# Conv-style attention with relative positions, two layers, on one Trainium2 core: the Sync queue reads q and k back after the maxima, xd and the output; score products one slot later

## The chip, the cores and the metric

The kernel runs on one core of one Trainium2 chip. The metric is the device time of one execution, in microseconds; lower is better.

## The reference

Two layers of the same shape, each `x = x + attention(groupnorm(x))`, on 64 samples of 14 x 14 tokens with 192 channels. Group normalisation takes 32 groups of 6 channels over the whole sample. The attention has 12 heads of 16 channels and a decomposed relative-position bias:

```python
q, k, v = (qkv[0], qkv[1], qkv[2])                 # qkv = gn(x) @ qkv_w + qkv_b
attn  = einsum('bqd,bkd->bqk', q * scale, k)
rel_h = einsum('bhwc,hkc->bhwk', q_as_grid, Rh)    # Rh[i,j] = rel_pos_h[i-j+H-1]
rel_w = einsum('bhwc,wkc->bhwk', q_as_grid, Rw)
attn  = softmax(attn + rel_h[..., :, None] + rel_w[..., None, :])
out   = (attn @ v) @ proj_w + proj_b
x     = x + out
```

Every product and sum above is computed for all 64 samples in both layers, and the second layer normalises what the first one has written.

## The kernel before, in words

One **unit** is one sample in one layer, so there are 128 units. The five engines each run their own program over all units. The work is software-pipelined by hand. Time is cut in iterations of 12 **slots**, one per head, and each step of a unit has a slot number counted from the unit's own iteration: slot number `at` is carried out in iteration `i` for unit `i - at // 12`, at position `at % 12`. On one engine, position and the order of the statements inside a position fix the order of instructions. Slots tie no engine to another; only semaphores do. So a slot number matters by the order that it gives on its queue.

What a unit goes through, with the lines of the profile:

- SP (SyncE's DMA queue) brings the sample in, `xa` (L395). PE transposes it, `xT` (L430), ACT and DVE copy it out and take the statistics (L739, L744), POOL turns them into scale and shift and writes the normalised sample as a high and a low half-precision part (`xn_hi`, `xn_lo`, L839, L844).
- PE forms q and k (`qk0`, `qk1` jobs, L413, slot 3), ACT and DVE write them as high and low parts `qk_hl` (L600, L730). SP writes them to DRAM (`qk_out`, L342: q first, then k) and reads them back in another layout into `q_st` and `k_st` (`q_in`, L370; `k_in`, L376, two transfers). v is formed in slot 10 (L413).
- PE forms the relative-position products (`rel0`, `rel1`, `rel2`, L474), ACT and DVE write them as `rel_hl`, and SP copies them into further rows of `q_st` (`rel`, L359, four transfers).
- From slot 28 on, one head per slot: PE forms the scores for the maxima (L525), DVE reduces them (`mx`, L718). After six heads PE transposes the maxima (`mT0`, `mT1`, L480), ACT writes them negated as `mrow` (L612), and SP puts them in the last row of `q_st` (`m0` and `m1`, L337). `m0` is for heads 0 to 5, `m1` for heads 6 to 11.
- From slot `EXP_AT` on, one head per slot: PE forms the score products again (L538), now with the maximum as one more row, and ACT takes the exponential (L588) into `probs`. Before head 0 PE waits for `m0`'s transfer, before head 6 for `m1`'s. PE multiplies probabilities and v (`PV_AT`, L557) in groups of four heads. The first group starts in slot 44 and waits for the exponential of head 3.
- The result is transposed (`ot`, L491, `oT`, L501), projected (`y`, L413, slot 60), and POOL adds the residual `xd` (L383) to it (`yo`, L855). SP writes `yo` out (`out`, L388). POOL's program has the statistics of the next unit (`mv`, L802, L805), which wait for DVE's L744, ahead of `yo` in each iteration.

PE works through its slots strictly in order. In one position it takes the maxima's product (L525), then the score product (L538), then the jobs of that position, then probabilities and v. ACT has in each position first the copy of L557's result, then the exponential, then the other copies.

SP's loop tests the steps in this order at each position: `m0`, `m1`, `rel`, `qk_out`, `q_in`, `k_in`, `xd`, `out`, `xa`. Each `dma_start` there stands behind its wait, and SP goes on only when that wait is over. With the numbers of before (`i` the iteration) SP's order in one iteration is: `xa(i+1)`, `m0(i-3)`, `qk_out(i)`, `q_in(i)`, `k_in(i)`, `xd(i-4)`, `out(i-5)`, `m1(i-3)`, `rel(i-1)`. `q_in` waits until q has landed in DRAM, `k_in` until k has, `out` for `yo` of its own unit, `m1` for ACT's `mrow`, `rel` for DVE's last part.

Of the kernel before, what the change touches and what calls it, by code (L numbers as in the profile page):

```python
# [71 lines left out]
def attention_kernel(nc, x_in, w_all, b_qk, b_rows, rel, onehot, lo_rows, ident_in, gmat_in, out):  # L72
    with ExitStack() as ctx:
# [42 lines left out]
        def pair(name, shape, dt=F32):  # L116
            return [sb(f"{name}{i}", shape, dt) for i in range(2)]

        xa = pair("xa", [HT, 2, C])
# [25 lines left out]
        xd = pair("xd", [HT, 2, C])  # L145
# [98 lines left out]


        LEAD, TAIL = 1, 6
        MAX_AT, EXP_AT = 28, 40

        PV_AT = {(0, 0): 44, (0, 1): 45, (1, 0): 49, (1, 1): 51, (2, 0): 54, (2, 1): 54}
        O_LATER = 1  # L250
# [22 lines left out]
        POOL_AT = {"mv": -11, "group": -3, "xn": -1, "xhi": 0, "xlo": 0, "y": 63}  # L273
        QK_TILES = ((0, 1), (2,))

        SP_AT = {"m0": 39, "m1": 46, "rel": 22, "qk_out": 3, "q_in": 3, "k_in": 4, "xd": 55, "out": 69, "xa": -12}

        def head_at(base, slot):

# [2 lines left out]
        def due(unit, slot, at):  # L282

            u = unit(at // HEADS)
            return u if at % HEADS == slot and active(u) else None
# [23 lines left out]
        def _(sp):  # L309
# [23 lines left out]
            def maxima(unit_, half):  # L333

                if active(unit_):
                    wait(sp, s_mrow, unit_.n * 2 + half + 1)
                    sp.dma_start(q_st[unit_.r][R_MAX:STACK, half * HH:half * HH + HH, :, :],  # L337
                                 mrow[unit_.r % 2][:, half, :]).then_inc(s_m[half][unit_.r], 16)

            def to_dram(unit_, dram, row, landed):  # L340

                sp.dma_start(dram[unit_.r].rearrange("l d h c t -> (d h) l (c t)"),  # L342
                             qk_hl[unit_.r % 2][row:row + HQ * HD, :, :, :]
                             .rearrange("p l c t -> p l (c t)")).then_inc(landed[unit_.r], 16)

            def iteration(unit, layer):
                for s in range(HEADS):
                    for half in range(2):
                        u = due(unit, s, SP_AT[f"m{half}"])
                        if u:  # L350
                            maxima(u, half)
                    u = due(unit, s, SP_AT["rel"])
                    if u:
                        wait(sp, s_rlo, u.n * 3 + 3)
                        for axis in range(2):
                            rows = RW if axis == 0 else 2 * SIDE
                            for half in range(2):
                                p, r0 = 64 * axis + 32 * half, R_REL + RW * axis
                                sp.dma_start(q_st[u.r][r0:r0 + rows, half * HH:half * HH + HH, :, :],  # L359
                                             rel_hl[u.r % 2][p:p + rows, :, :]).then_inc(s_rel[u.r], 16)  # L360
                    u = due(unit, s, SP_AT["qk_out"])
                    if u:
                        wait(sp, s_qklo, u.n * 2 + 2)
                        to_dram(u, q_dram, 0, s_qd)
                        to_dram(u, k_dram, HQ * HD, s_kd)
                    u = due(unit, s, SP_AT["q_in"])
                    if u:
# [3 lines left out]
                          .then_inc(s_qst[u.r], 16)  # L371
                    u = due(unit, s, SP_AT["k_in"])
                    if u:
                        wait_dma(sp, s_kd, u)
                        for part in range(2):
                            sp.dma_start(k_st[u.r][2 * HD * part:2 * HD * part + 2 * HD, :, :],  # L376
                                         k_dram[u.r].rearrange("l d h c t -> d l (h c t)"))\
                              .then_inc(s_kst[u.r], 16)
                    u = due(unit, s, SP_AT["xd"])
                    if u:  # L380
# [533 lines left out]
```

## Time and profile before

| | us |
|---|---|
| median of 3 runs (2547.81 to 2555.18) | 2550.9 |
| the profiled execution | 2526.95 |
| its span, first to last instruction | 2525.2 |
| PE busy | 2178.0 (86%) |
| DVE busy | 1434.6 (57%) |
| ACT busy | 1419.7 (56%) |
| POOL busy | 715.6 (28%) |
| mean granted TensorE clock | 0.879 |

A profile's row for a group of instructions gives the line, the engine, the operation, the tiles, how often it ran, how long it was busy and what ended the idle time before it. A row of a timeline gives start, duration, engine, line, operation and tiles, and in brackets the idle time before it with what ended it. PE's durations are modelled: the start of the next matmul tells more than the duration of the last. The granted clock is 1.00 at 2.4 GHz and 0.50 at 1.2 GHz.

### The profile page before, as it was taken

The page shows a single profiled execution, that of the slowest core. Times are in us where ns is not written, and L with a number is a line of the kernel's source. Part 1 is how long each engine was busy: PE and PEld are TensorE (multiplying, and loading weights), DVE is VectorE, ACT ScalarE, POOL GpSimd, SP SyncE. Part 2 cuts the span into 40 slices and gives each one's busy share as a digit, 9 for nine tenths or more (in the row PEclk, how much of TensorE's full clock was granted, in tenths as well). Part 3 has the DMA queues.
Part 4 walks back from the last instruction along what each step waited for, and adds up shares of the span by engine and source line. Part 5 has one row for each costly group of instructions (what it writes and reads, how often), then busy time and mean ns, then how long its engine had stood idle before and what let it go on. Part 6 is the DMA issues. An engine that isn't in the chain of part 4 may idle for free.

```text
span 2525.2 us, 86928 instructions
## 1 busy us (share of the span) xinstructions
PE 2178.0 (86%) x35072; PEld 1815.6 (72%) x35072; DVE 1434.6 (57%) x3540; ACT 1419.7 (56%) x3329; POOL 715.6 (28%) x1796
## 2 busy tenths in 40 slices
PE   2888888888988888988988888988888888898897
PEld 2777777777777777776777777777777777777776
DVE  5655555565555556555555555655555655565554
ACT  1556555555655555655555555555555655565555
POOL 1322322232223223223222322332223222323220
PEclk9989888888888989989888988888888988998888
DMA  2433333333333334333333433333333333333331
GB/s 49 106 85 84 93 85 85 83 98 87 80 85 90 92 81 100 86 85 98 84 80 85 101 81 80 90 92 85 80 90 95 85 87 81 96 90 88 89 78 52
DMA packets 170599, 217.20 MB, mean 86 GB/s; under 512 B 29783, under 2 KB 138072, under 8 KB 170202
## 3 DMA queue, kind: packets, MB, share of 16 engines
q1 hardware_dynamic: 170202, 211.64, 33.8%
q8 instruction: 282, 4.62, 0.8%
q14 instruction: 115, 0.94, 0.1%
HBM read 117.00 MB, written 57.80 MB: 69 GB/s over the span
## 4 chain that ended last, share of the span: by engine, by line
PE 42%; DMA 30%; SPq 16%; DVE 5%; issue 3%; ACT 3%; POOL 1%; POOLq 0%; ACTq 0%
PE ps_m L413 21%; DMA q_st<-mrow 14%; DMA k_dram<-qk_hl 10%; PE ps_sc L538 8%; SPq L376 7%; PE ps_max L525 6%; DMA q_dram<-qk_hl 5%; DVE qk_hl L730 4%; SPq L383 3%; PE ps_m L501 3%; SPq L388 3%; PE ps_o L557 3%; ACT qk_hl L600 2%; SPq L342 2%; SPq L370 1%
## 5 line engine op out<-in xcount | busy, mean ns | idle before, releaser
L718 DVE TENSOR_REDUCE mx<-ps_max 98x2 f32<-98x392 f32 x1536 | 836.8, 562 | 433.1 <-PE ps_max L525 431.4
L588 ACT ACTIVATE probs<-ps_sc 98x392 f32<-98x392 f32 x1536 | 727.7, 495 | 536.6 <-PE ps_sc L538 505.5
L538 PE MATMUL ps_sc<-q_st,k_st 125*98 125x196 f16 x3072 | 568.7, 270 | 286.4 <-DMA q_st<-mrow 286.1
L525 PE MATMUL ps_max<-k_st,q_st 124*98 124x196 f16 x3072 | 580.4, 273 | 0.9 <-DVE mx L718 0.7
L538 PEld LDWEIGHTS ps_sc<-q_st,k_st 125*98 125x98 f16 x3072 | 352.7, 137 | 314.3 <-DMA q_st<-mrow 311.6
L525 PEld LDWEIGHTS ps_max<-k_st,q_st 124*98 124x98 f16 x3072 | 324.5, 135 | 204.7 <-issue 198.3
L802 POOL TENSOR_TENSOR msq<-mv 96x2 f32<-96x2 f32 x128 | 24.6, 192 | 1538.2 <-DVE mv L744 1538.2
L557 PE MATMUL ps_o<-probs,v_st 98*32 98x196 f32 x6144 | 389.0, 340 | 0.5 <-ACT o_sb L578 0.5
L636 ACT ACTIVATE rel_hi<-ps_m,is_lo 128x504 f16<-128x504 f32 (+1 forms) x384 | 225.8, 588 | 149.4 <-PE ps_m L474 137.3
L776 DVE TENSOR_TENSOR oT_lo<-ps_m,oT_hi 96x392 f16<-96x392 f32 x128 | 71.9, 562 | 415.5 <-ACT oT_hi L618 415.5
L474 PE MATMUL ps_m<-q_st,rel_st 64*32 64x36 f16 (+1 forms) x14336 | 238.2, 209 | 1.9 <-DVE rel_hl L769 1.6
L769 DVE TENSOR_TENSOR rel_hl<-ps_m,rel_hi 128x504 f16<-128x504 f32 (+1 forms) x384 | 216.2, 563 | 23.2 <-ACT rel_hi L636 6.5
L474 PEld LDWEIGHTS ps_m<-q_st,rel_st 64*32 64x32 f16 x14336 | 191.5, 101 | 46.1 <-DVE rel_hl L769 2.3
L413 PE MATMUL ps_m<-xn_hi,w_hi 98*128 98x196 f16 (+1 forms) x768 | 193.2, 252 | 10.4 <-POOL xn_lo L844 10.4
L413 PE MATMUL ps_m<-xn_lo,w_hi 96*128 96x196 f16 x768 | 192.2, 250 | 0.0
L730 DVE TENSOR_TENSOR qk_hl<-ps_m,qk_hl 128x392 f16<-128x392 f32 (+1 forms) x256 | 107.2, 460 | 149.5 <-ACT qk_hl L600 149.5
L413 PE MATMUL ps_m<-xn_hi,w_lo 96*128 96x196 f16 x768 | 191.6, 249 | 0.0
L557 PEld LDWEIGHTS ps_o<-probs,v_st 98*32 98x32 f32 x6144 | 134.4, 108 | 73.2 <-issue 1.0
L413 PE MATMUL ps_m<-w_hi,xn_lo 96*98 96x192 f16 x512 | 176.0, 344 | 0.0
L413 PE MATMUL ps_m<-w_lo,xn_hi 96*98 96x192 f16 x512 | 175.8, 343 | 0.0
L413 PE MATMUL ps_m<-w_hi,xn_hi 98*98 98x192 f16 (+1 forms) x512 | 175.6, 343 | 0.0
L413 PE MATMUL ps_m<-w_hi,oT_hi 98*98 98x192 f16 (+1 forms) x512 | 154.0, 301 | 2.7 <-DVE oT_lo L776 2.7
(72 smaller groups left out, 3338.3 us busy)
## 6 DMA issues: line engine op xcount, KB each, us to landing
q_st<-q_dram SPq DMA_DIRECT2D x128, 294.0 KB, 3.9
k_st<-k_dram SPq DMA_DIRECT2D x256, 147.0 KB, 3.9
q_dram<-qk_hl SPq DMA_DIRECT2D x128, 147.0 KB, 2.6
k_dram<-qk_hl SPq DMA_DIRECT2D x128, 147.0 KB, 2.7
q_st<-rel_hl SPq DMA_DIRECT2D x256, 73.5 KB
q_st<-rel_hl SPq DMA_DIRECT2D x256, 64.3 KB
xa<-in_x SPq DMA_DIRECT2D x64, 147.0 KB
xd<-in_x SPq DMA_DIRECT2D x64, 147.0 KB
```

Source lines behind the costliest of these rows:

```text
L376: sp.dma_start(k_st[u.r][2 * HD * part:2 * HD * part + 2 * HD, :, :], k_dram[u.r].rearrange("l d h c t -> d l (h c t)"))\
L383: sp.dma_start(xd[u.r % 2][:, :, :], tokens(src[bass.ds(at, 1)])).then_inc(s_xd[u.r], 16)
L413: last = nc.tensor.matmul(dst, weights(a, c, k), moving(b, c, k), start=n == 0, stop=n == len(terms) - 1)
L474: last = nc.tensor.matmul(to, rel_st[:, lay, axis, w:w + RW], q, start=True, stop=True)
L525: last = nc.tensor.matmul(ps_max[head % 2][0:HT, h * TOK:h * TOK + TOK], q_st[u.r][0:R_MAX, head, h, :], k_st[u.r][0:R_MAX, head, :], star ...
L538: last = nc.tensor.matmul(ps_sc[head % 2][0:HT, kt * TOK:kt * TOK + TOK], k_st[u.r][0:STACK, head, kt * HT:kt * HT + HT], q_st[u.r][0:STAC ...
L557: last = nc.tensor.matmul(ps_o[32 * j:32 * j + 32, 0:TOK], v_st[u.r][:, kt, head_of(head), :], p[:, kt, :], start=kt == 0, stop=kt == 1)
L588: nc.scalar.activation(probs[head][:, :, :], ps_sc[head % 2][0:HT, 0:2 * TOK].rearrange("p (k t) -> p k t", k=2), ACT.Exp, scale=1.0 / (QS ...
L636: nc.scalar.activation(rel_part(rel_hi[u.r % 2], n), rel_bank(n), ACT.Identity, scale=is_lo[:, 0:1]).then_inc(s_rhi, 1)
L718: nc.vector.reduce_max(mx[u.r % 2][:, head, :], ps_max[head % 2][0:HT, 0:2 * TOK].rearrange("p (q k) -> p q k", q=2), axis=AX.X).then_inc( ...
L730: nc.vector.tensor_tensor(qk_hl[u.r % 2][:, 1, at, :], ps_m[BANK[f"qk{j}"]][:, 0:len(tiles) * TOK].rearrange("p (c t) -> p c t", t=TOK), q ...
L769: nc.vector.tensor_tensor(rel_part(rel_hl[u.r % 2], n), rel_bank(n), rel_part(rel_hi[u.r % 2], n), ALU.subtract).then_inc(s_rlo, 1)
```

## The change

Only slot numbers change. SP's order becomes `xa(i+1)`, `m0(i-3)`, `qk_out(i)`, `xd(i-4)`, `out(i-5)`, `m1(i-3)`, `q_in(i)`, `k_in(i)`, `rel(i-1)`. `m0` keeps its place in the order, and so do `qk_out`, `rel` and `xa`. The score products and exponentials of each head are one slot later on PE and ACT. No instruction is added or removed.

```diff
-        MAX_AT, EXP_AT = 28, 40
+        MAX_AT, EXP_AT = 28, 41
...
-        SP_AT = {"m0": 39, "m1": 46, "rel": 22, "qk_out": 3, "q_in": 3, "k_in": 4, "xd": 55, "out": 69, "xa": -12}
+        SP_AT = {"m0": 37, "m1": 43, "rel": 22, "qk_out": 4, "q_in": 8, "k_in": 8, "xd": 54, "out": 66, "xa": -12}
```

## Rows read from the trace of the kernel before

**Rows 1.** Waits over the whole span: engine, line, releaser: total us, times, longest us

```profile
PE ps_sc L538 <- DMA q_st<-mrow: 286.1, 125, 3.7
```

**Rows 2.** Span and mean granted clock of the core

```profile
core 0: 2525.2 us, clock 0.879
```

**Rows 3.** The chain that ended last, one iteration: start us, us, what

```profile
1209.63 2.80 DMA k_dram<-qk_hl
...
1215.53 2.19 DMA q_st<-mrow
```

**Rows 4.** PE timeline, an iteration at the full clock, 860 to 879 us

```profile
860.42 0.37 PE L538 MATMUL ps_sc<-q_st,k_st 125*98 125x196 f16 x2 [2.03 <-DMA q_st<-mrow]
...
866.95 0.50 PE L430 MATMUL ps_m<-ident,xa 98*96 98x98 f32 x4
...
877.12 0.37 PE L538 MATMUL ps_sc<-q_st,k_st 125*98 125x196 f16 x2 [1.75 <-DMA q_st<-mrow]
...
878.66 0.33 PE L525 MATMUL ps_max<-k_st,q_st 124*98 124x196 f16 x2
```

**Rows 5.** One-us windows, 1216 to 1225 us: PE busy (matmuls), granted clock, DMA share, GB/s

```profile
1216.00:1217.00 1.00, 0.27 (x2) 1.00 0.81 266
...
1218.00:1219.00 1.00, 1.00 (x8) 0.50 0.32 78
...
1224.00:1225.00 1.00, 1.00 (x14) 0.78 0.02 2
```

**Rows 6.** SP's own timeline in the same iteration as rows 4

```profile
868.02 0.68 SPq L342 DMA_DIRECT2D q_dram<-qk_hl  x1
868.74 0.64 SPq L342 DMA_DIRECT2D k_dram<-qk_hl  x1
870.63 0.56 SPq L370 DMA_DIRECT2D q_st<-q_dram  x1
871.32 1.41 SPq L376 DMA_DIRECT2D k_st<-k_dram  x2
872.77 0.57 SPq L383 DMA_DIRECT2D xd<-in_x  x1
873.39 0.41 SPq L388 DMA_DIRECT2D x<-yo  x1
873.85 0.81 SPq L337 DMA_DIRECT2D q_st<-mrow  x1
874.71 2.90 SPq L359 DMA_DIRECT2D q_st<-rel_hl  x4
877.65 0.55 SPq L395 DMA_DIRECT2D xa<-in_x  x1
```

**Rows 7.** POOL timeline of the iteration after, whose L430 on PE started at 883.65

```profile
887.31 1.00 POOL L855 TENSOR_TENSOR yo<-yr,xd 98x384 f32<-98x384 f32 x1
```

**Rows 8.** The page's group of the exponentials: busy, mean ns, idle before

```profile
L588 ACT ACTIVATE probs<-ps_sc 98x392 f32<-98x392 f32 x1536 | 727.7, 495 | 536.6 <-PE ps_sc L538 505.5
```

**Rows 9.** PE timeline around slot 44: what stands between head 4's scores and L557

```profile
1232.49 1.18 PE L491 MATMUL ps_m<-ident,o_sb 128*98 128x68 f32 x12
...
1234.04 0.54 PE L557 MATMUL ps_o<-probs,v_st 98*32 98x196 f32 x8
```

**Rows 10.** SP's issues of k's read-back, 147 KB each: ns and landing us, min/median/max

```profile
L376 SPq DMA_DIRECT2D k_st<-k_dram x256: 552/593/1724, 50.3 to 2466.9; - x128
...
DMA to landing us min/median/max: 2.8/3.9/5.0
```

**Rows 11.** SP's issues of rel: ns min/median/max

```profile
L359 SPq DMA_DIRECT2D q_st<-rel_hl x512: 536/783/1449, 64.4 to 2488.9; - x171
```

**Rows 12.** Half-us window behind rows 6 (same columns as rows 5)

```profile
880.50:881.00 0.50, 0.50 (x10) 1.00 0.00 0
```

**Rows 13.** PE timeline: first and last of the 125 waits of rows 1

```profile
93.68 0.37 PE L538 MATMUL ps_sc<-q_st,k_st 125*98 125x196 f16 x2 [1.02 <-DMA q_st<-mrow]
...
2471.93 0.56 PE L538 MATMUL ps_sc<-q_st,k_st 125*98 125x196 f16 x2 [3.39 <-DMA q_st<-mrow]
```

## The prediction, made before the changed kernel had run

> **What bounds the kernel now.** I read the totals of the waits first. PE has one large wait: the score products of head 6 wait for the transfer of `m1`, the second row of maxima, 125 times, 286.1 us in all, 2.3 us a unit [rows 1]. PE is busy for 86% of the span and every other engine for 57% or less, so PE's own order of work is the frame and this wait is the hole in it.
>
> The chain that ended last says why `m1` is late. One iteration of it runs from the q and k products over `qk_hl` and SP's write to DRAM, the landing of k there (2.80 us), the read-backs, `xd`, `out` and `m1` to the landing of `m1` (2.19 us), and only then into L538 [rows 3, 4]. The maxima are not late. SP stands in front of them, because `q_in` and `k_in` wait for landings and `m1` is behind them.
>
> SP's timeline shows this in numbers. I count from the start of `xT` on PE (L430, 866.95, [rows 4]), which follows the q and k products directly, and call it zero. `qk_out` is issued from 1.07 to 2.43, `q_in` starts at 3.68 when q has landed, `k_in` at 4.37, `xd` at 5.82, `out` at 6.44, `m1` at 6.90, `rel` at 7.76 and `xa` at 10.70 [rows 6]. L538 of head 6 starts at 10.17, after 1.75 us of waiting, that is, PE was there at 8.42 [rows 4].
>
> The windows show a second price. The clock is granted in full while PE stands still and falls to half right behind it: 1.00 at 1216, 0.50 at 1218, back only during 1224 [rows 5]. The mean of 0.879 [rows 2] puts 2 x 0.121 x 2525.2 = 611 us at 1.2 GHz. In the one-us windows of the whole span I find falls only behind such a wait, never in the busy stretches between two of them. Some waits are followed by none, and one such case is in [rows 4]. There one iteration is 877.12 - 860.42 = 16.70 us, of which 1.75 is the wait: **14.95 us of PE work at the full clock**. The average iteration between the first and the last wait is (2471.93 - 93.68) / 124 = 19.18 us [rows 13]. The difference of 4.23 us is 2.3 us of waiting and 1.9 us of slow clock.
>
> **The change, part by part.**
>
> *SP's order.* Nothing is added, so the issues keep their durations and only their order is new. `xd` can go at 2.47 (its own wait is for a residual sum two units back, long over) and is done at 3.04. `out` now waits for something: `yo` of its unit ends on POOL at 888.31, which is 4.66 after that iteration's `xT` [rows 7]. So `out` is issued from 4.70 to 5.11 and `m1` from 5.15 to 5.96. Its landing after the start of the issue took 3.27 us in one iteration (873.85 to 877.12, [rows 4, 6]), and 2.19 in another [rows 3]. That gives a landing between 7.4 and 8.4. I take 7.9, between them; both ends go into the range.
>
> *Behind `m1`.* `q_in` goes at 6.0, and q landed before 3.7, so its old wait is gone. `k_in` runs from 6.6 to 8.1. k's landing in DRAM, from 1.79 with 2.8 us [rows 3], is over at 4.6; with the 5.0 us that is the longest landing of a 147 KB transfer [rows 10] it would be over at 6.8, 0.2 late. The four `rel` transfers take 2.90 and end at 11.0, `xa` at 11.6. Against before, `xa` starts at 11.05 instead of 10.70, 0.35 later. First users: `q_in` is needed by `rel0` in the next iteration, over 5 us after its landing; `k_in` an iteration after that; `rel` by the next maxima's head 0 behind `xT`, at about 15.9. The tightest is `xa`, needed at 14.95 by the next `xT`. Its landing isn't listed. The DMA engines stand still at 880.5 [rows 12], 2.85 us after `xa`'s issue at 877.65 [rows 6], so it lands by 13.9, with 1.05 to spare. With 5.0 us [rows 10] it would be 16.05, 1.1 late. I take 2.85, since it is of this transfer itself, and keep the other end. `m0`, behind `xa`, lands by 11.6 + 3.3 = 14.9 and is needed at about 16.4.
>
> *Scores one slot later.* PE now has one more score product, `oT` and the v product in front of head 6. Everything from head 6's scores to the next maxima's product takes 878.66 - 877.12 = 1.54 us [rows 4], and one more maxima's product follows (0.17). So PE needs `m1` at 8.42 + 1.54 + 0.17 = 10.1 instead of 8.42. Against the landing of 7.4 to 8.4 that is 1.7 to 2.7 us of slack, while with the new order alone it would be 0 to 1.0. The slot costs little otherwise. In slot 44 the scores of head 3, not 4, now stand in front of L557, which needs that head's exponential of 0.495 us [rows 8]. Between them PE still has `ot` and `rel2`, 1234.04 - 1232.49 = 1.55 us [rows 9]. If that cover were gone, the cost would be some 0.5 us in each of 128 units, 64 us. The pipeline's end is one slot longer, 0 to 1 us once.
>
> *The sum.* Up to the first wait's start: 93.68 - 1.02 = 92.7. Then 124 x 14.95 = 1853.8. Behind the last one, 2525.2 - 2471.93 = 53.3, less 3.2 for a slow stretch behind it like the one in [rows 5] (6.4 us at half the clock, from 1218 to 1224.4): 50.1. Half a us for the slot. Together **1997.1 of span**, 1999 with the 1.75 us around the span. The profiled execution (2526.95) lies 24 us, 0.9%, under the median of 2550.9. I expect most of that spread to come from the waits and the clock and little to stay; with a few us for scattered late transfers I forecast **2004**. A cross-check from the totals gives 2525.2 - 286.1 - 611/2 = 1934. It is too low, as part of the slow clock falls into the waits, where it costs nothing, but it marks the low end.
>
> **The clock.** The fall comes behind the wait [rows 5], and without a fall PE needs 14.95 us [rows 4]. By these rows the clock comes back with the wait gone. The Trainium skill (TensorE: Matmul & The Clock Gate, "HAM oscillation — how this bites in real kernels") ties the fall to an idle gap longer than 1.75 us; by that rule the waits would not be its cause, and removing them would not cure it.
>
> **The rivals.**
>
> *The clock doesn't return.* Only the wait goes: 2525.2 - 286.1 + 1.75 = 2241. For it speaks that the cause of a fall is inferred, and that not every wait has one. Against it, that no fall in the trace stands away from a wait. Chance 0.06. That is the time that the sentence of the Trainium skill above would give.
>
> *The wait moves to `xa`.* SP's order now closes a loop: `xa` releases `xT`, its statistics release POOL's `yo`, this releases `out`, and behind `out` stand `m1`, `q_in`, `k_in`, `rel` and the next `xa`. The loop is 13.9 us by my sums, only 1.05 under PE's 14.95. Issues and landings that are a little longer when the same traffic fits into 15 instead of 19 us make some iterations end on it. At 16.05 in every iteration it is 124 x 1.1 = 136 us, 2140; short waits that also halve the clock could bring it to 2230. Chance 0.12.
>
> *Slower.* The same loop at its worst. `k_in` with both issues at 1.72 (2.0 more than in [rows 6], by [rows 10]), `rel` with four at 1.45 (2.9 more, [rows 11]) and a landing of 5.0 (2.15 more) make 13.9 + 7.05 = 20.9 us, 124 x 20.9 + 143 + 2 = 2737. It decides from 19.18 us on, 5.3 us above my loop. What speaks for it is that `m1`'s wait and `out`'s wait now stand in front of five issues that used to go before them. Against it, that these maxima were single issues and not whole iterations. Chance 0.04.
>
> *No change.* Something that I have not seen holds `m1` at 10.2 to 12, say ACT's `mrow`. The rows show `m1` going the moment `out` is issued. Chance 0.03.
>
> **How the numbers follow.** The forecast has a chance of 0.75 and its own range is 1965 to 2060. The range for 8 in 10 adds the nearer half of the `xa` case: 1965 to 2140. A measurement here tells about 0.3% (8 us) from no change. Faster by more: 0.75 + 0.12 + 0.06 = 0.93. Within: 0.03. Slower: 0.04.
>
> **What would show it.** Right: the wait of L538 for `mrow` falls from 286.1 us to under 20; the clock's mean is above 0.97; xT to xT is 15.0 us; on SP `out` follows `yo` and `m1` follows at once, at 5.2; `q_in` has no wait. Wrong: a wait of L430 for `xa`, or of L525 for `rel`, of more than 50 us in all (the loop); a clock near 0.88 without waits (the rule); a wait of L557 for the exponential (the slot's cover); `m1` waiting for `mrow`.

## The result, and the profile after

The changed kernel takes **1974.85 us** (median of 4 runs, 1972.92 to 1978.24) against 2553.04 us for the kernel before on the same chip. The ratio is 0.7736, 95% interval 0.7715 to 0.7758. The forecast was 2004 us. The profiled execution took 1975.75 us, with a span of 1973.9.

The page of the changed kernel, its totals and the shares of the chain that ended last:

```profile
span 1973.9 us, 86928 instructions
PE 1911.7 (97%) x35072; PEld 1568.6 (79%) x35072; DVE 1424.8 (72%) x3540; ACT 1387.7 (70%) x3329; POOL 716.1 (36%) x1796
...
PE 92%; DVE 2%; SPq 2%; DMA 2%; issue 1%; POOL 1%; ACT 0%; POOLq 0%; ACTq 0%
```

The same line of chain shares in the kernel before:

```profile
PE 42%; DMA 30%; SPq 16%; DVE 5%; issue 3%; ACT 3%; POOL 1%; POOLq 0%; ACTq 0%
```

With the same instructions as before, transfers and SP's issues were 46% of the chain and are now 4%. PE is the chain, with 92% of it. DVE, ACT and POOL do the same work in a shorter span, so their shares rise and their busy times hardly move. PE's own busy time falls by 266 us though no product was taken away. That is the clock, 0.997 on average where it was 0.879 [rows 2]:

```profile
core 0: 1973.9 us, clock 0.997
```

From 90 to 1960 us the full clock is granted throughout; the one slow stretch lies in the last units. The row has the columns of [rows 5], the granted clock is its 1.00:

```profile
90.00:1960.00 1870.00, 1866.93 (x34508) 1.00 0.46 113
```

In the waits of PE, the row of [rows 1] is gone. What PE waits for now, the largest first:

```profile
PE ps_m L430 <- DVE yo L707: 33.2, 1, 33.2
...
PE ps_m L413 <- POOL xn_lo L844: 10.4, 3, 5.1
...
PE ps_m L436 <- POOL mv L805: 5.5, 2, 3.5
```

The first is the setup and the others belong to the first units. On SP a wait for `yo` has taken the place of the wait for q's landing. Before:

```profile
SPq L370 <- DMA q_dram<-qk_hl: 192.3, 128, 2.9
```

After:

```profile
SPq L388 <- POOL yo L855: 201.0, 127, 11.0
...
SPq L370 <- DMA q_dram<-qk_hl: 6.5, 3, 3.1
```

`out` waits for `yo` in nearly every unit, 1.6 us each, which costs nothing here, since PE doesn't wait for what is behind it. SP's timeline of one iteration, as [rows 6] had it before:

```profile
909.88 0.68 SPq L342 DMA_DIRECT2D q_dram<-qk_hl  x1
910.60 0.64 SPq L342 DMA_DIRECT2D k_dram<-qk_hl  x1
911.28 0.59 SPq L383 DMA_DIRECT2D xd<-in_x  x1
913.50 0.33 SPq L388 DMA_DIRECT2D x<-yo  x1
913.87 0.79 SPq L337 DMA_DIRECT2D q_st<-mrow  x1
914.70 0.58 SPq L370 DMA_DIRECT2D q_st<-q_dram  x1
915.33 1.23 SPq L376 DMA_DIRECT2D k_st<-k_dram  x2
916.60 3.33 SPq L359 DMA_DIRECT2D q_st<-rel_hl  x4
919.98 0.55 SPq L395 DMA_DIRECT2D xa<-in_x  x1
```

`xT` (L430) starts on PE at 908.81. Counted from there, `out` goes at 4.69 (4.70 was forecast), `m1` at 5.06 (5.15), `q_in` at 5.89 (6.0), `xa` at 11.17 (11.05). PE's timeline around head 6 (L538 at 918.75), as in [rows 4]:

```profile
908.81 0.50 PE L430 MATMUL ps_m<-ident,xa 98*96 98x98 f32 x4
...
916.87 0.37 PE L525 MATMUL ps_max<-k_st,q_st 124*98 124x196 f16 x2
917.07 0.33 PE L538 MATMUL ps_sc<-q_st,k_st 125*98 125x196 f16 x2
...
918.75 0.33 PE L538 MATMUL ps_sc<-q_st,k_st 125*98 125x196 f16 x2
...
923.56 0.50 PE L430 MATMUL ps_m<-ident,xa 98*96 98x98 f32 x4
```

Head 6 comes at 9.94 (10.1 was forecast), without a wait. From `xT` to `xT` it is **14.75 us** (14.77 on average), against 19.2 on average before, and this hardly varies: between the 11th unit and the last but two, 90% of the distances lie from 14.74 to 14.92.

### The profile page after: what moved, and what is told of

It is laid out like the page before. It is cut to its first block, busy times and chain, and to the rows that moved or that the text cites. A ratio compares the mean times of both kernels' runs of the same rounds, so it can differ in the third digit from the quotient of the medians.

```text
span 1973.9 us, 86928 instructions
## 1 busy us (share of the span) xinstructions
PE 1911.7 (97%) x35072; PEld 1568.6 (79%) x35072; DVE 1424.8 (72%) x3540; ACT 1387.7 (70%) x3329; POOL 716.1 (36%) x1796
## 4 chain that ended last, share of the span: by engine, by line
PE 92%; DVE 2%; SPq 2%; DMA 2%; issue 1%; POOL 1%; ACT 0%; POOLq 0%; ACTq 0%
PE ps_m L413 23%; PE ps_max L525 17%; PE ps_o L557 17%; PE ps_sc L538 13%; PE ps_m L474 10%; PE ps_m L491 6%; PE ps_m L430 2%; PE ps_m L501 2%; PE ps_m L480 2%; SPq L359 1%; DMA xa<-x 1%; PE ps_m L436 1%; DVE mx L718 0%; DMA xa<-in_x 0%; DVE k_st L675 0%
## 5 line engine op out<-in xcount | busy, mean ns | idle before, releaser
L588 ACT ACTIVATE probs<-ps_sc 98x392 f32<-98x392 f32 x1536 | 717.7, 496 | 162.2 <-PE ps_sc L538 116.9
L525 PE MATMUL ps_max<-k_st,q_st 124*98 124x196 f16 x3072 | 539.2, 257 | 0.7 <-DVE mx L718 0.6
L538 PE MATMUL ps_sc<-q_st,k_st 125*98 125x196 f16 x3072 | 511.3, 247 | 0.3 <-ACT probs L588 0.2
L525 PEld LDWEIGHTS ps_max<-k_st,q_st 124*98 124x98 f16 x3072 | 290.1, 124 | 201.7 <-issue 197.7
L557 PE MATMUL ps_o<-probs,v_st 98*32 98x196 f32 x6144 | 389.0, 340 | 0.8 <-ACT probs L588 0.6
L538 PEld LDWEIGHTS ps_sc<-q_st,k_st 125*98 125x98 f16 x3072 | 320.6, 124 | 3.0 <-ACT probs L588 1.9
L557 PEld LDWEIGHTS ps_o<-probs,v_st 98*32 98x32 f32 x6144 | 134.5, 108 | 73.3 <-issue 1.4
L600 ACT CAST qk_hl<-ps_m 128x392 f16<-128x392 f32 (+1 forms) x256 | 103.6, 405 | 86.2 <-PE ps_m L413 83.1
L491 PE MATMUL ps_m<-ident,o_sb 128*98 128x68 f32 x1536 | 151.5, 247 | 0.4 <-ACT o_sb L578 0.4
L855 POOL TENSOR_TENSOR yo<-yr,xd 98x384 f32<-98x384 f32 x128 | 128.2, 1002 | 55.9 <-ACT yr L650 55.9
L491 PEld LDWEIGHTS ps_m<-ident,o_sb 128*98 128x98 f32 x1536 | 143.6, 167 | 1.0 <-ACT o_sb L578 1.0
L578 ACT COPY o_sb<-ps_o 128x196 f32<-128x196 f32 x384 | 123.9, 323 | 10.8 <-PE ps_o L557 1.6
```

The source lines that it names most:

```text
L491: last = nc.tensor.matmul(ps[0:HT, at:at + HG * (HD + 1)], o_sb[p2][:, g, h * HT:h * HT + HT], ident[:, :].rearrange("p (j x) -> p j x", x ...
L525: last = nc.tensor.matmul(ps_max[head % 2][0:HT, h * TOK:h * TOK + TOK], q_st[u.r][0:R_MAX, head, h, :], k_st[u.r][0:R_MAX, head, :], star ...
L538: last = nc.tensor.matmul(ps_sc[head % 2][0:HT, kt * TOK:kt * TOK + TOK], k_st[u.r][0:STACK, head, kt * HT:kt * HT + HT], q_st[u.r][0:STAC ...
L557: last = nc.tensor.matmul(ps_o[32 * j:32 * j + 32, 0:TOK], v_st[u.r][:, kt, head_of(head), :], p[:, kt, :], start=kt == 0, stop=kt == 1)
L578: nc.scalar.copy(o_sb[u.r % 2][:, g, :].rearrange("p (k r b) -> p k r b", r=2, b=SIDE), ps_o[:, 0:TOK].rearrange("p (k b r) -> p k r b", r ...
L588: nc.scalar.activation(probs[head][:, :, :], ps_sc[head % 2][0:HT, 0:2 * TOK].rearrange("p (k t) -> p k t", k=2), ACT.Exp, scale=1.0 / (QS ...
```

## The experiments

Ten runs. Times are medians, beside the kernel before on the same chip.

### The order alone

The new order of SP, with the scores back in slot 40. The lines shown are against the changed kernel.

```diff
-        MAX_AT, EXP_AT = 28, 41
+        MAX_AT, EXP_AT = 28, 40
```

> The new SP order with the score products back in slot 40. In the changed kernel m1 is issued 5.06 us after the start of xT (913.87 against 908.81), and PE would come to head 6's scores at about 8.25. With a landing 2.2 to 3.3 us after the issue, m1 is there at 7.3 to 8.4. My theory (the order takes the wait away, the slot only gives margin): 1975 to 2010 us, the wait of L538 for mrow under 20 us in all, clock above 0.98. Rival (the slot is needed): landings above 8.25 are common, each wait brings the slow clock with it, and the time is 2100 us or more with a clock under 0.96.

Measured: 1985.62 us, ratio 0.7747 (0.772 to 0.7774), clock 0.996. Its wait for the maxima:

```profile
PE ps_sc L538 <- DMA q_st<-mrow: 6.2, 15, 0.7
```

The order alone brings nearly all of the gain. `m1` is late in 15 of 128 units and by 0.7 us at most, a little outside the calculated slack of 0 to 1.0 us, which had no late one. In these units it was issued on time, at 5.05 to 5.07, and landed 3.5 to 4.1 us later. The first figure of the changed kernel, 11 us lower, was taken on another chip, so both were run again side by side:

> The changed kernel unaltered, beside the next run on the same chip: 1970 to 1985 us. It is the mark for the slot's share.

> The new SP order with the scores in slot 40, as in the first experiment, now against the changed kernel on the same chip. Theory: the slot takes away the few waits that the order leaves (15 waits, 6.2 us in that profile, and slow clock behind some), worth 5 to 15 us; this kernel is that much slower than the changed one. Rival: the 11 us between the first two measurements are the chips', and both kernels are equal within 4 us.

Measured: the changed kernel 1974.15 us (1973.04 to 1976.13), the order alone 1981.51 us (1979.78 to 1984.66). The ranges don't overlap. The slot is worth 7.4 us, 0.4%, and the order the remaining 563 of 570 us. The slow clock that I expected behind some of the late landings isn't there. Between 90 and 1960 us, where all of them lie, the first of these profiles shows the full clock:

```profile
90.00:1960.00 1870.00, 1860.94 (x34380) 1.00 0.46 113
```

Its two slow stretches are at 74.5 us, in the first units, and at the end. The 7.4 us fit the late landings themselves: 14 waits with 5.8 us in the second of these profiles.

### Which part of the order

Only `m1` ahead of the read-backs, `xd` and `out` behind them as in the kernel before, scores in slot 41 (against the changed kernel):

```diff
-        SP_AT = {... "m1": 43, ... "q_in": 8, "k_in": 8, "xd": 54, "out": 66, ...}
+        SP_AT = {... "m1": 43, ... "q_in": 8, "k_in": 8, "xd": 57, "out": 69, ...}
```

> Scores in slot 41, m1 right behind qk_out, then q_in, k_in, xd and out as before. m1 then waits only for mrow, at about 3.7 us after xT's start, and is issued at about 3.8; q_in at 4.6, k_in 5.2 to 6.6, xd and out to 7.7, rel to 10.6, xa at 10.6. My theory (only m1's place ahead of the read-backs counts): 1970 to 1980 us, the same as the changed kernel. Rival (xd and output ahead are needed too): over 2000 us, with waits of POOL or of L430.

Measured: 1978.57 us (1976.85 to 1981.37), ratio 0.7722 (0.7695 to 0.7749), clock 0.998, no wait for the maxima.

Only `xd` and `out` ahead, `m1` behind the read-backs, scores in slot 40 (against the changed kernel):

```diff
-        MAX_AT, EXP_AT = 28, 41
+        MAX_AT, EXP_AT = 28, 40
...
-        SP_AT = {... "m1": 43, ...}
+        SP_AT = {... "m1": 46, ...}
```

> Scores in slot 40, xd and out ahead of q_in and k_in, but m1 still behind k_in. out ends at 5.1 us after xT's start, q_in at 5.7, k_in at 7.2, m1 is issued at 7.2 to 8.0 and lands at about 10.1, as in the kernel before. My theory (m1's place is what counts): 2450 to 2600 us, the wait for mrow over 200 us and the clock at 0.86 to 0.90. Rival (the place of xd and out is what counts): under 2100 us.

Measured: 2529.68 us (two runs), ratio 0.9871 (0.9814 to 0.9928), clock 0.890. Its wait for the maxima:

```profile
PE ps_sc L538 <- DMA q_st<-mrow: 289.4, 125, 3.5
```

This is the kernel before in all that counts, though `xd` and `out` have moved and SP's wait for q's landing has shrunk from 192.3 to 9.5 us. In place of q's landing SP now waits for `yo`, and `m1` is issued at 7.5 us from `xT` at the median, against 7.6 before. The 1.3% isn't settled by two runs: the kernel before itself took 2522 to 2569 us beside them. So `m1`'s place is the change. Moving `xd` and `out` as well was not needed; `m1` moved alone with the scores in slot 40 was not run. `m1` can go at 3.72, since it then doesn't stand behind `yo`, but PE has no use for it so early.

### Is it the idle wait that makes the clock fall?

The slow clock stands only behind the wait in the kernel before. To part the two losses, PE was given work without use in front of the wait. The wait for the exponential of the head before goes ahead of them, as their bank must be free. Nothing else was touched, so the wait for `m1` stays where it is, only not idle. The sixteen products are written to a bank that head 6's scores overwrite next.

```diff
+                        wait(pe, s_p, u.n * HEADS + head - 1)
+                        if head == HH:
+                            for _ in range(16):
+                                nc.tensor.matmul(ps_sc[head % 2][:, 0:TOK], w_hi[0:CB, 0, 0, 0:128],
+                                                 w_hi[0:CB, 0, 0, 0:TOK], start=True, stop=True)
                         if head % HH == 0:
                             wait_dma(pe, s_m[head // HH], u)
-                        wait(pe, s_p, u.n * HEADS + head - 1)
```

> The kernel before, in which PE runs 16 more matmuls of 196 columns (about 82 ns each at the full clock, 1.3 us, results overwritten unread) in front of head 6's wait for m1, so that most of the wait is filled with work of no use. SP's order is that of before. My theory (the idle wait itself makes the clock fall): the clock stays up, above 0.97, each iteration is bounded by SP's chain at 16.5 to 17.2 us, and the time is 143 + 124 x 17 = 2250 us, some 12% faster with more work. Rival (the slow clock has another cause, as the rule with the longer gap has it): the clock stays at about 0.88 and the time at 2520 to 2560 us, or it grows by up to 124 x 1.3 = 160 us.

Measured: 2357.94 us (2355.84 to 2362.07), ratio 0.9205 (0.9167 to 0.9244). **Eight per cent faster with more work.** The clock was 0.978. Its wait (lines behind the addition are four higher):

```profile
PE ps_sc L542 <- DMA q_st<-mrow: 142.6, 121, 2.9
```

The direction and the clock are as the theory has them, and the rival's unchanged clock is out. The size was missed by 108 us. I had taken SP's chain at 17.0 us, the length of the quick iterations in the trace before, which are those with early landings and no slow stretch. In this run `xT` to `xT` is 17.80 on average: where PE waits for `m1`, it is there at 10.95 at the median, and not at the 10.17 of [rows 4]. Then with 28 products:

> The kernel before with 28 instead of 16 matmuls without use in front of the wait, 2.3 us of work. With 16 of them the profile still had 142.6 us of waits and a clock of 0.978. m1 lands at 10.98 us after xT's start at the median there, and PE would come to the wait at 8.25 + 2.3 = 10.6. My theory: waits under 90 us, clock above 0.99, and the time bounded by max(SP's chain, PE) at 2320 to 2400 us, near the 2358 of 16 matmuls although 127 x 1 = 127 us of work is added. Rival (added work costs its time): 2460 us or more.

Measured: 2334.3 us (two runs), ratio 0.9196 (0.9014 to 0.9379), clock 0.997.

```profile
PE ps_sc L542 <- DMA q_st<-mrow: 48.6, 68, 1.6
```

Twelve more matmuls in each unit and no more time. The clock is now that of the changed kernel, while SP's chain is that of the kernel before. And the changed kernel with the first sixteen:

> The changed kernel with the same 16 matmuls without use in front of head 6's wait. If PE's own work is now the only bound, each unit is 16 x 0.083 = 1.3 us longer: 1974 + 127 x 1.3 = 2140 us, clock above 0.99. If another loop had been close behind PE and PE had slack in it, the time would be under 2100. The difference to the kernel before with the same 16 matmuls (2358 us) is then the price of SP's chain without most of the slow clock.

Measured: 2136.78 us (two runs, 2134.37 and 2139.18), clock 0.998.

Forecast 2140. The distance from `xT` to `xT` goes from 14.75 to 16.03, 1.28 us for sixteen matmuls of 80 ns. In the changed kernel PE's order is the bound to the last tenth of a microsecond, and nothing else is close enough to hide added work. The same sixteen matmuls cost the changed kernel 162 us and save the kernel before some 200.

These runs split the gain. From 2334 (waits mostly filled, clock full) to 1974 is 360 us, the price of SP's chain. From 2550 (the kernel before beside that run, median of 2514, 2550 and 2550) to 2334 is 216 us, the price of the slow clock. The line between them isn't sharp: `xT` to `xT` never went under 17.09 us in the run with 28 products, which is PE's 14.75 plus the 2.3 of added work, so some of its units are bound by that work. The chain's share is at most 360 and the clock's at least 216 (180 by the fastest of the three).

The trace of the kernel before gives the same split directly. Over its 116 middle units, PE takes 8.42 us from `xT` to the wait, waits 2.30, and takes 8.50 from head 6's scores to the next `xT`. With 28 products, at the full clock, this last part is 6.53. So the slow clock costs 1.97 us a unit, some 245 in all. With 286 us of waits, and some 21 that each wait's overlap adds (125 x 0.17, worked out further down), that makes 552, and the spans differ by 551.

### How near is the loop over xa?

The second rival was that SP's loop from one `xa` to the next becomes the bound. To measure its slack, SP issues one or three transfers of 4 bytes more behind `k_in`, to places that nobody reads:

```diff
+                        for e in range(3):
+                            at = 3 * u.n + e
+                            sp.dma_start(spare[0:1, at:at + 1], ident_in[0:1, 0:1]).then_inc(s_spare, 16)
```

> The changed kernel with one more small transfer (4 bytes, to a place that nobody reads) issued by SP behind k_in in each unit. It lengthens SP's loop from xa to the next xa by one issue, 0.4 to 0.7 us. In the changed kernel xa is issued 11.22 us after xT's start at the median (11.85 at the 95th percentile), and the next xT comes at 14.75. Theory of the prediction (about 1 us of slack at the median): waits of L430 for xa in a quarter of the units, 0 to 0.4 us each, 1975 to 2010 us. Rival (no slack is left): every unit is 0.4 to 0.7 us longer, 2030 to 2060 us.

> The same with three more transfers, 1.2 to 2.1 us of issues. Theory: the slack of about 1 us is used up, and the loop of xa bounds each iteration: 124 x (0.2 to 1.1) more, 2000 to 2110 us, with waits of L430 (or of L525 for rel) for transfers in most units. If each such wait also brought the slow clock, the time would be above 2200 us. Rival (the landing of xa is much earlier than I think, with 2 us or more of slack): 1975 to 1985 us.

Measured: with one, 1980.21 us (1976.93 to 1987.26), 6 us over the changed kernel on the same chip; its profile has four waits of `xT` for `xa`, not the quarter of the units that I expected. With three, 2018.58 us (2005.09 to 2023.06), 44 us over it. With three, `xa` is issued at 12.24 at the median instead of 11.22, and PE waits for it (lines are six higher here):

```profile
PE ps_m L436 <- DMA xa<-in_x: 7.0, 14, 1.6
PE ps_m L436 <- DMA xa<-x: 5.2, 14, 0.7
```

These are 28 units, where I expected most. But a short delay shows as no wait, as the products ahead of `xT` start 0.08 us apart and are modelled as 0.25 long, and 69 of 118 distances from `xT` to `xT` are above 14.80, against 10 in the changed kernel. One issue more (0.4 us) costs next to nothing, three (1.0 us) begin to cost. So the loop has between 0.4 and 1.0 us of slack at the median, and the 1.05 of the prediction was the right size. In that profile `xT` to `xT` is 14.95 on average, 0.2 over the changed kernel, with a clock of 0.995. The timed runs at 2015 to 2021 us of span had clocks of 0.987 to 0.991 and were 12 to 18 us longer than the profiled one. The profiled run has one slow stretch ahead of the last units, 10.2 us long, and it follows the longest of its waits for `xa` (two windows and between them the row of the wait; the clock is 1.00 in the first and 0.50 in the second):

```profile
99.00:100.00 1.00, 0.00 (x0) 1.00 0.04 8
...
100.13 0.54 PE L436 MATMUL ps_m<-ident,xa 98*96 98x98 f32 x4 [1.64 <-DMA xa<-in_x]
...
101.00:102.00 1.00, 1.00 (x12) 0.50 0.97 214
```

That the slower runs had more such stretches fits their clocks, but is not shown: they have no trace.

## Why the prediction was right, and where it was off

**What bound the kernel.** Right. `m1` stood behind the read-backs; moving it ahead of them, and that alone, gives the time (1978.57 with `m1` moved alone in the order and the scores in slot 41, 2529.68 with `xd` and `out` moved but not `m1`, and the scores in slot 40).

**SP's order.** Every start but one is right within 0.15 us. `rel` starts 0.3 earlier than the 8.1 of the prediction, as `k_in` took 1.23 us, and takes 3.33 instead of 2.90; that `xa` comes out right is in part these two errors cancelling. `m1`'s landing isn't in the trace where nobody waits for it. In the run with the order alone, PE's waits end at 8.59 to 9.12 from `xT`, so in those few units it lands beyond the 8.4 that I gave as the later end. That end came from two iterations. Over all 125 waits of the kernel before, PE goes on 1.9 to 4.4 us after `m1`'s issue, which from 5.06 on gives up to 9.4. The slot's margin, up to 9.94, covers this.

**The slot.** By the prediction the order alone would leave 0 to 1.0 us of slack and the slot adds 1.7 to it. That margin is worth 7.4 us. The cover of the first group of L557 held: the page of after has that line waiting 0.6 us for exponentials in the whole span.

**The sum.** 2004 was forecast, 1975 measured. Two terms make the 29 us. The mis-sized one is PE's work at the full clock: 14.95 us a unit in the prediction, and 14.76 on average from head 6 at 93.01 to the same place 124 units on, at 1923.34. That is 124 x 0.19 = 23.5 us. The start (93.0 for 92.7) and the end (50.6, as forecast with the slot) came out. The working subtracted the wait as the trace gives it, and this is counted from the modelled end of the last product. Before the wait of [rows 4] stood:

```profile
875.00 0.37 PE L525 MATMUL ps_max<-k_st,q_st 124*98 124x196 f16 x2
```

875.00 + 0.37 = 875.37, from where the 1.75 us run. But where there is no wait, the next product starts 0.20 behind that one (916.87 to 917.07 above), not 0.37, since the end of one overlaps the start of the next. A wait costs that overlap too, 0.17 us, and the sum left it in PE's work: 21 of the 23.5 us. The other 5 us were the allowance for scattered late transfers. They are rare in the trace: `xT` has waits of 0.16 and 0.71 us for `xa` and no more beyond the start.

**The clock.** Right. Its mean went from 0.879 to 0.997, and the runs with added products show that the idle wait is the cause. One detail of the prediction was misread: the clock doesn't wait for PE to start again. Of the 104 slow stretches before, 77 begin inside a wait, that of [rows 5] too, and 26 at most 1.5 us behind its end; the last one is at the end of the program. The other 22 of the 125 waits have no slow stretch. They lasted 1.0 to 2.5 us and those with one 1.3 to 3.7, so the length alone doesn't tell which; what does stays open. The Trainium skill (TensorE: Matmul & The Clock Gate, "HAM oscillation — how this bites in real kernels") ties the fall to longer idle gaps than nearly all of these; here the measurement decides: with waits of 1.0 to 3.7 us in each unit the clock was 0.879, and with the same waits mostly filled it was 0.997.

**The rivals.** That the clock doesn't return (2241) fell with the result itself. That `m1` would be held by ACT's `mrow` fell too: `m1` is issued at 5.06, right behind `out`. The loop over `xa` exists and is tight, but not reached. The slower case needed 5.3 us more on that loop; the longest distance between two `xT` behind the first units was 15.6 us. The spread of the kernel before goes with the clock, as I expected: beside the last runs it took 2514.40 us with a clock of 0.885 and 2549.95 with 0.873. By the way of the prediction (2 x 0.012 x 2530 us at 1.2 GHz, half of it lost) that is 30 of the 36 us. The changed kernel, which has neither waits nor slow clock, varies by 0.3%.

## What to carry to other kernels

In a queue written out by hand, an item that waits for a landing blocks everything behind it, so put what is ready and has an early user in front of it; here one transfer of 2.3 KB behind the read-backs cost 22% of the time, the slow clock included. Where a short wait of TensorE returns in every iteration, look at the granted clock behind it: the wait's own total understates its price, here 286 us of some 570. Before moving something, close the loop of the new order (here `xa` to `xa`) and compare its length with the engine that is to become the bound.

## What the runs showed of the hardware

Idle waits of 1.0 to 3.7 us (2.15 at the median), one in each 19 us, left TensorE at a mean clock of 0.879; the same kernel with part of the waits filled by 16 products without use had 0.978 and, with 28 of them, 0.997, and ran 8% faster. Fifteen waits of up to 0.7 us, in the run with the order alone, brought no slow stretch. A wait in a PE row is counted from a modelled end, and cost 0.17 us more than it says here, behind matmuls of 196 columns at the full clock. Three issues of 4 bytes each took SP 1.01 us (in the run with three more), a third of a microsecond each, and moved `xa` by as much: 12.24 - 11.22 = 1.02.

```profile
918.20 1.01 SPq L383 DMA_DIRECT2D spare<-in_ident  x3
```
